# Grouped-norm, sign and 3x3 convolution on one core: the last pair's output taken bank by bank, and two waits and a warm-up moved near the start

## The reference, cut to what matters

```python
def reference(x, W, beta, v, bias):            # x: 32 images, 56 x 56, 32 channels, fp32
    xn = groupnorm(x, 32 groups)               # mean and variance per image and channel
    # W: 3x3x32x32, replaced by a least-squares sum of 5 sign filters
    B = sign(W - mean(W) + u[m] * std(W)), m = 0..4
    alpha = solve(B.T @ B, B.T @ W);  W_eff = sum_m alpha[m] * B[m]
    out = 0
    for n in range(3):
        A = sign(clip(xn + v[n], 0, 1) - 0.5)  # +1 or -1
        out += beta[n] * (conv3x3(A, W_eff) + sum(alpha) * bias[n])
    return x + out
```

## Time and profile before

| | us |
|---|---|
| median of 3 runs | 198.26 |
| the three runs | 198.69, 195.89, 198.26 |
| time of the profiled execution | 197.91 |
| its span, first to last instruction | 195.0 |
| TensorE busy | 174.5 (89%) |
| VectorE busy | 162.1 (83%) |
| ScalarE busy | 153.9 (79%) |
| GpSimd busy | 58.1 (30%) |
| mean granted TensorE clock | 0.965 |

### The profile page before, as it was taken

The page is one execution under the profiler, slowest core; times in us unless marked ns, Lnnn a source line. Parts: engine busy times, 40 slices in busy tenths (PEclk is TensorE's granted clock), DMA queues, the critical chain, the costliest instruction groups (busy, mean ns, idle before and its releaser), DMA issues.

```text
span 195.0 us, 4830 instructions
## 1 busy us (share of the span) xinstructions
PE 174.5 (89%) x1840; PEld 135.2 (69%) x1840; DVE 162.1 (83%) x406; ACT 153.9 (79%) x220; POOL 58.1 (30%) x74
## 2 busy tenths in 40 slices
PE   1897499399999999989999999999999999999960
PEld 1686486287777777767777777877787867768660
DVE  4579976979789999999899999899989999884332
ACT  2719949999789898989898989998989896953210
POOL 6264010506060505060515151424141424161000
PEclk9999669879999999999999999999999999999996
DMA  5999991054496989899978989889873838687525
GB/s 148 241 238 236 250 225 26 0 126 144 125 252 183 246 267 239 246 226 303 252 229 231 278 226 278 235 257 241 269 221 115 222 118 233 175 231 185 171 71 165
DMA packets 20349, 39.60 MB, mean 203 GB/s; under 512 B 9063, under 2 KB 9063, under 8 KB 20327
## 3 DMA queue, kind: packets, MB, share of 16 engines
q1 hardware_dynamic: 20016, 39.27, 74.2%
q10 hardware_dynamic: 310, 0.04, 0.1%
HBM read 13.15 MB, written 12.85 MB: 133 GB/s over the span
## 4 chain that ended last, share of the span: by engine, by line
PE 63%; DVE 15%; DMA 10%; ACT 7%; SPq 2%; issue 2%; DVEq 0%
PE conv_ps L805 34%; PE y_ps L827 11%; DMA s_odd<-s_even 9%; PE x_ps L755 6%; DVE raw_stats L597 4%; DVE y_nat L588 4%; ACT signs L359 4%; PE conv_ps L813 3%; DVE s_even L650 2%; PE conv_ps L808 2%; PE conv_ps L893 2%; PE conv_ps L775 2%; SPq L219 2%; ACT x_ch L354 1%; ACT filt L390 1%
## 5 line engine op out<-in xcount | busy, mean ns | idle before, releaser
L805 PE MATMUL conv_ps<-s_even,w_mm 128*64 128x448 f16 (+1 forms) x576 | 104.6, 336 | 1.6 <-DMA s_odd<-s_even 1.4
L808 PE MATMUL conv_ps<-s_odd,w_mm 128*64 128x448 f16 (+2 forms) x576 | 104.6, 324 | 0.0
L359 ACT ACTIVATE signs<-x_ch,neg_thr 128x784 f16<-128x784 f32 x96 | 85.4, 939 | 0.5
L805 PEld LDWEIGHTS conv_ps<-s_even,w_mm 128*64 128x64 f16 x576 | 61.1, 111 | 30.7 <-issue 6.2
L808 PEld LDWEIGHTS conv_ps<-s_odd,w_mm 128*64 128x64 f16 x576 | 61.1, 111 | 0.0
L322 POOL TENSOR_SCALAR lo_part<-signs,ratio_lo 128x1568 f16<-128x1568 f16 x15 | 23.6, 1572 | 99.5 <-DVE half_hi L643 92.5
L588 DVE SCALAR_TENSOR_TENSOR y_nat<-y_ps,y_const,x_nat 112x1024 f32<-112x1024 f32 (+1 forms) x32 | 36.8, 1149 | 11.7 <-PE y_ps L827 11.3
L372 ACT ACTIVATE y_ch<-conv_ps,y_scale 128x896 f32<-128x896 f32 (+1 forms) x32 | 29.1, 908 | 19.8 <-PE conv_ps L813 12.5
L827 PE MATMUL y_ps<-ident,y_ch 128*112 128x128 f32 x224 | 30.9, 278 | 1.5 <-DVE y_nat L588 1.5
L597 DVE BATCH_NORM_STATS2 raw_stats<-x_ch 128x6 f32<-128x448 f32 (+1 forms) x64 | 31.6, 555 | 0.8 <-ACT x_ch L354 0.8
L755 PE MATMUL x_ps<-ident,x_nat 112*128 112x112 f32 x192 | 25.4, 275 | 4.9 <-ACT x_ch L354 3.1
(11 more groups left out here) (119 smaller groups left out, 121.9 us busy)
## 6 DMA issues: line engine op xcount, KB each, us to landing
x_nat<-in_x SPq DMA_DIRECT2D x16, 448.0 KB, 5.8
out<-y_nat SPq DMA_DIRECT2D x16, 448.0 KB, 5.0
s_odd<-s_even SPq DMA_DIRECT2D x32, 203.0 KB, 3.3
s_odd<-s_even SPq DMA_DIRECT2D x32, 188.5 KB, 3.6
x_nat<-in_x SPq DMA_DIRECT2D x16, 336.0 KB, 4.8
out<-y_nat SPq DMA_DIRECT2D x16, 322.0 KB, 2.9
s_odd<-s_even SPq DMA_DIRECT2D x16, 29.0 KB, 3.1
x_nat<-in_x SPq DMA_DIRECT2D x16, 14.0 KB, 6.0
```

What stands on the lines that cost most here:

```text
L359: act.activation(signs[q % 2][:, n, :, a, :], x_ch[q % CH_SLOTS][:, :, a, :], ACT.Sign, bias=neg_thr[q % 2][:, n, a:a + 1]).then_inc(signe ...
L805: last = nc.tensor.matmul(low[:, 0:n * ROWS], wt, s_even[b][:, part, r0:r0 + 2 * n, t:t + H], start=first, stop=end)
L808: last = nc.tensor.matmul(high[:, 0:m * ROWS], wt, s_odd[b][:, part, r0:r0 + 2 * m, t:t + H], start=first, stop=end and not at_edge)
```

## The change

The last pair's conv B is computed with its second bank first. Its two banks are scaled out, transposed, added and stored one by one; the transposes of the last pair's conv A go to `x_ps`, which is free by then, and stand between the two banks. The transposes of (4,0) wait for seven copies instead of eight. ScalarE does `sign(1, 2)` ahead of `copy_in(3, 0)`. The warm-up ahead of the second conv A is gone, and the one after the transposes of (2,0) is doubled.

```diff
+LAST = PAIRS - 1
+LAST_BANKS = (1, 0)
...
-                if real(p):
+                if real(p) and p != LAST:
                     store(p, 1)
...
+            y = y_nat[LAST % 2]
+            stored = y_stored[LAST % 2]
+            sp.wait_ge(last_added, 1)
+            sp.dma_start(out_pairs[LAST][:, 45 * C:], y[:, 44 * C:55 * C]).then_inc(stored, 16)
+            sp.dma_start(out_pairs[LAST][:, 0:C], y[:, 55 * C:]).then_inc(stored, 16)
+            sp.wait_ge(last_added, 2)
+            sp.dma_start(out_pairs[LAST][:, 33 * C:45 * C], y[:, 32 * C:44 * C]).then_inc(stored, 16)
...
+            def scale_last(k):
+                j = LAST_BANKS[k]
+                n = half_bank(1)
+                act.wait_ge(last_conv, k + 1)
+                act.activation(y_ch[1][:, j * n:(j + 1) * n], conv_ps[1][:, j, 0:n], ACT.Copy, scale=y_scale[:])\
+                    .then_inc(last_scaled, 1)
...
-                if real(p):
+                if p == LAST:
+                    act.wait_ge(y_transposed, 2 * LAST)
+                    scale_last(0)
+                    scale_last(1)
+                elif real(p):
                     scale_out(p, 1)
...
+            sign(1, 2)
             copy_in(3, 0)
-            sign(1, 2)
...
+            def add_last(k):
+                j = LAST_BANKS[k]
+                n = PER_BANK[1] * 128
+                at = OUT_COLS[1].start + j * n
+                dve.wait_ge(last_transposed, k + 1)
+                stt(y_nat[LAST % 2][:, at:at + n], y_ps[0:ROWS, j, 0:n], y_const[0:ROWS, :],
+                    x_nat[LAST % X_SLOTS][:, C + at:C + at + n], ALU.add, ALU.add).then_inc(last_added, 1)
...
-                    add_x(p, 0)
+                    add_x(p, 0, x_ps if p == LAST else y_ps)
...
-                if real(p):
+                if p == LAST:
+                    add_last(0)
+                    add_last(1)
+                elif real(p):
                     add_x(p, 1)
...
                 if f == 0:
-                    if p == 1:
-                        warm_up(conv_ps[0], 10)
                     pe.wait_ge(hi_made, p + 1)
...
+            def bring_out_last(k):
+                j = LAST_BANKS[k]
+                pe.wait_ge(last_scaled, k + 1)
+                if k == 0:
+                    pe.wait_ge(y_added, 2 * LAST)
+                for i in range(PER_BANK[1]):
+                    at = j * PER_BANK[1] + i
+                    last = nc.tensor.transpose(y_ps[0:ROWS, j, i * 128:(i + 1) * 128],
+                                               y_ch[1][:, at * ROWS:(at + 1) * ROWS], ident[:])
+                last.then_inc(last_transposed, 1)
...
             def step(p):
                 r, t = p + 3, p + 4
+                if p == LAST:
+                    convolve(p, 1, LAST_BANKS[0:1], last_conv)
+                    pe.wait_ge(x_copied, 2 * PAIRS)
+                    bring_out(p, 0, x_ps)
+                    convolve(p, 1, LAST_BANKS[1:2], last_conv)
+                    bring_out_last(0)
+                    bring_out_last(1)
+                    return
...
                 if real(t + 1):
-                    bring_in(t + 1, 0)
+                    bring_in(t + 1, 0, x_ps, 7 if p == -1 else None)
...
             warm_up()
+            warm_up()
             bring_in(2, 1, y_ps, 4)
```

20 lines of the change are left out of this document (12 added, 8 removed).

## The result

The changed kernel takes 194.35 us (median of 4 runs, 193.95 to 195.17), against 197.55 us of the kernel before (median of 4, 195.89 to 198.69). The ratio is 0.987, with a 95% interval of 0.982 to 0.992. It was timed twice more among the experiments, each time against the kernel before on the same chip, and traced each time: ratios 0.989 (0.983 to 0.995) and 0.985 (0.981 to 0.990). So it is faster, by some 1.3%, which is more than the measurement's uncertainty and less than 2%. The profiled execution took 193.95 us, with a span of 191.5 us; before these were 197.91 and 195.0.

What follows compares the result with a forecast made beforehand. The prediction took TensorE to bound the kernel, busy 9.67 us of a middle pair's 9.67, with VectorE close at 9.30. From 197.91, less 1.7 (start) and 1.8 (end), it forecast 194.4 us; range for 8 in 10: 193.0 to 196.5.

Steps and rivals of the forecast that it cites:

- The wait for one copy less: Start, transposes of (4,0): they start some 2.6 us earlier; the wait moves behind conv B, leaving about 1.3 us.
- The order of sign and copy: Start, ScalarE: the copy of (3,0) now comes last, so pair 2's small matmul slips up to 0.24 us.
- The first conv A gains nothing: Start, doubled warm-up step: the upper part's second shifted copy lands 6.5 us after issue, at 30.04, so no gain.
- The doubled warm-up: Start: four extra matmuls cost nothing while TensorE waits for a copy; worth 0 to 0.24 us, taken as 0.
- The warm-up taken away: Start: the second conv A, held by late shifted copies, ends at 48.3 instead of 50.14, 1.8 us won.
- The clock: Start, behind a 2.5 us idle: a low clock inside conv A costs 1.5 us; the whole start is taken as 1.7.
- The first rival: Start: the lower clock reaches the second conv A, the start is worth 0.5 us, time 195.6; chance 18%.
- The middle: Middle pairs: VectorE, busy 9.30 us against TensorE's 9.67, can follow, so nothing is taken off the start's gain.
- The second rival: Middle: waits for shifted copies take the start's gain back, only the end's 1.8 us stays, time 196.1; chance 12%.
- The prediction's own sign of being wrong: Middle: pairs longer than 9.8 us on average would be one sign that the prediction is wrong.
- The end: Last pair: bank-by-bank work with the long add under the second bank lands the last store at 192.8, 1.8 us won.
- Slower by eleven waits for copies: Middle, rival: conv A waits for copies in all eleven pairs that still load x, time 199.6; chance 4%.

Runs made afterwards that it cites:

- the kernel that keeps the clock at 0.996 to 1.000: Changed kernel with the copy of (3,0) ahead of the signs and 11 warm-up matmuls in TensorE's wait behind conv B of pair 0: 193.26 us, ratio 0.978.

## Why the prediction was right, and where its terms were off

The forecast was 194.4 us. The median is 194.35, so the number hit more closely than the reasons deserve. The sum was made against the profiled execution of before (197.91), which lies 0.36 us above the median of 197.55 that the new runs gave; between the medians the gain is 3.2 us where 3.5 were forecast, and the ratios give 2.2 to 2.9 us over the three sets. Taken singly, the start measured 1.3 us where 1.7 were forecast, and the end 1.2 where 1.8 were.

- **The wait for one copy less: right.** 3.10 became 0.39 and conv B of pair 0 took 2.8 us at full clock. The wait moved behind it: 3.05 us, where 2.5 were expected, since the small matmul came at 41.27 as forecast (41.2 and the slip) and conv B ended at 38.2 and not at 38.6. Half of that difference is an error of adding: 34.6 + 1.04 + 2.76 is 38.4. The experiment with eight copies shows what the step didn't say: with the warm-up gone, this edit is worth nothing of its own, because the shifted copies are late next.
- **The order of sign and copy: the direction right, the term mis-sized.** The term was 0.24 us of slip. It was priced with the first conv A where it stood in the trace of before (30.13), and the same prediction held that it could not come earlier. It came at 29.40, and at 28.70 in another execution, and the copy then took what was won: the small matmul of pair 2 stayed at 33.71, with a wait of 0.68 us. With the order put back the time is 1.3 us less in one set and 1.9 in the other. The step that failed is the sentence "The first conv A gains nothing". It was read from one landing, the upper part's second shifted copy 6.5 us after its issue; in the changed kernel's three executions that copy landed after 5.0, 3.9 and 5.0 us, and TensorE could start as soon as it was free.
- **The doubled warm-up: worth 0, right in the outcome.** 195.41 us with four matmuls and 195.19 with eight. It didn't reliably hold the clock up: from 23.00 to 26.50 the clock was 0.52, 0.54 and 1.00 in the changed kernel's three executions.
- **The warm-up taken away: right.** The second conv A was to start near 44 and end near 48.3; it started at 43.95 and ended at 48.13. One detail was not foreseen: the upper part's copies were late as well (0.83 us in front of the conv A, then 0.42 inside).
- **The clock: right for this execution, and by luck.** The second conv A ran at 1.00 behind a wait of 3.05 us. The Trainium skill, page "TensorE: Matmul & The Clock Gate", section "Why this matters for your kernels", warns of the lower clock behind such gaps; this trace doesn't show it, and seven others with the same wait do (below). The first rival, the lower clock in the second conv A, was thus a matter of the execution. Its price on TensorE was right, 1.2 us forecast: from the small matmul of pair 2 to the end of the second conv A it was 15.7 us in the two traces in which the clock was at 0.50 until past 45 us (the first run with the copy first, and the one with the transposes behind both banks), and 14.3 to 14.4 in those at full clock. In the other five with a low clock behind this wait it ended by about 45 us or sooner, and in the four of them without the ten warm-ups the way was 14.45 to 14.66: as the prediction said, the wait for the copies covered nearly all. In the time it doesn't show: the kernel that keeps the clock at 0.996 to 1.000 is no faster.
- **The middle: the term of 0 was too small.** In the first execution it is nearly right. From the scaling of the second pair's conv A to that of the thirteenth's it is 107.7 us for eleven pairs (48.9 to 156.6), 9.79 a pair; before it was 108.3 (50.2 to 158.5), 9.84. Of a lead of 1.9 us at the end of the second conv A 1.7 arrived at the last one, which is just what I took for the start. That was luck. In the other two executions of the same kernel the eleven pairs took 108.5 and 109.4 us, 9.86 and 9.94 a pair, and 0.7 and 1.0 us arrived; with the start alone 0.5 of 2.4 us did. So the middle gave back 0.2 to 1.9 us, where the step "Does the middle keep it?" took nothing off, and this fits the 1.3 us that the start alone measured. The waits for shifted copies rose from 1.4 us in four to 2.6 in five, 2.9 in seven and 2.8 in five; that they are the whole of it isn't shown. The second rival was right in part. All these leads are against the one trace of the kernel before, whose own scatter isn't known. The prediction's own sign of being wrong, pairs of over 9.8 us on average, was no sign: the kernel before had 9.84.
- **The end: right.** Forecast 1.8 us; in the traces the ladder to the last issue is 1.6 us shorter and the landing 0.2. Scaling one bank took 0.54 (0.53 forecast), three transposes 0.54 (0.45), a short add 0.66 (0.63), and from the last conv matmul to the last issue it was 2.0 us, as forecast. The half with the end alone measured 1.2 us.
- **Slower by eleven waits for copies:** did not come; there were five to seven. The run with copies issued by GpSimd shows that such a thing can happen: thirteen waits, 8.5 us, and a kernel slower than before.

## What to carry to other kernels

When TensorE is made faster at one place, look again at every order on the engines that feed it: an order that cost nothing with TensorE late can cost a wait once TensorE is early. Here one swapped pair of lines made a wait of up to 0.7 us, and without it the kernel was 1.3 and 1.9 us faster in two sets of runs. A lead won at the start is not yet a gain at the end: read it at both places, and in more than one execution. Two edits that aim at the same stall are not to be added; price each with the other already made. At the end of a kernel, look for the longest step that needs only what is ready earlier, and put it under the last matmuls.

## What the hardware showed that I had not expected

- **The same wait, another clock.** TensorE waits 3.05 or 3.06 us for the copy of (4,0), behind conv B of pair 0, in ten of the traces here. From 38 to 45 us the granted clock stayed at 1.00 in three of them, the changed kernel's first and second profiled execution and that with one early warm-up. In the other seven it fell: in the changed kernel's third (0.53 from 42 to 45), with the start only (0.51), with ten warm-ups back (0.57), with the transposes behind both banks (0.50), with copies issued by GpSimd (0.50) and in both with the copy first (0.50, and 0.70 from 38 to 42). The changed kernel's three executions run the same program. So one trace doesn't tell whether such a wait costs the clock; with the wait filled it stayed at 1.00 in the one trace taken, and the mean over the span was 0.996 or more in all six executions.
- **The issuer's price.** The same three copies within the chip's on-chip memory took 3.7, 5.0 and 4.8 us from issue to landing when GpSimd issued them, and 3.65, 3.6 and 3.1 when SyncE did, and the kernel was some 6 us slower. How much of it is the issuer and how much what SyncE sends meanwhile wasn't tried.
- **An issue's length.** The last pair's 14 KB store took SyncE 0.43 to 0.46 us to issue in most traces, and 0.84 us in the one with the transposes behind both banks, on the way to the last store. In the trace with one early warm-up two others took 1.45 and 1.50 us (at 123.16 and 179.11), where the rest took 0.42 to 0.46. What made it longer wasn't tried.
